# Cross attention: where the low part of the context rows is made, and when the sums of probabilities are taken

## The reference, cut to what matters

```
qx = _ln(qx, qxln_w, qxln_b)                      # 16 heads of 128, in 8 groups of 2
kvx = jnp.einsum('bsi,oi->bso', cond, w_kv_x)     # cond is the context
kx, vx = jnp.split(kvx, 2, axis=-1)
kx = _ln(kx.reshape(b, sc, g, d), kxln_w, kxln_b)
xout = _gqa(qx, kx, vx).reshape(b, s, nh * d)     # softmax(qx kx^T / sqrt(d)) vx
```

## Time and profile before

| | us |
|---|---|
| median of 3 runs | 2561.54 (2557.67 to 2563.57) |
| the profiled execution, its own time | 2560.54 |
| its span in the profile | 2558.5 |
| cross attention in it, first fold to last store, about | 1117 to 2315 |

### The profile page before, as it was taken

One profiled execution on the slowest core, in us unless ns is written; L12 is line 12 of the kernel. 1 busy time (PEld: TensorE's weight loads), 2 busy tenths in 40 slices (PEclk: granted clock), 3 DMA queues, 4 the chain that ended last, 5 costly groups with the idle time before them and its releaser, 6 DMA issues. The chain is left out here.

```text
span 2558.5 us, 38343 instructions
## 1 busy us (share of the span) xinstructions
PE 2341.7 (92%) x12603; PEld 2045.3 (80%) x12603; DVE 2019.6 (79%) x3952; ACT 1088.3 (43%) x1849; POOL 919.4 (36%) x640
## 2 busy tenths in 40 slices
PE   7999999999984788859999999999999999986797
PEld 6777777779983666658888888988888888976797
DVE  8999987877757887848888888888888888871487
ACT  1000001108855666614544554455545454554332
POOL 5455100200012344424545544555455444570000
PEclk9999999999996888879999999999999999997899
DMA  9667623517624010042222212222222112106211
GB/s 389 263 266 274 240 99 145 191 66 255 220 98 144 37 44 36 29 135 77 84 74 79 69 46 80 83 80 69 74 83 71 63 57 83 61 4 162 56 55 39
DMA packets 143384, 286.66 MB, mean 112 GB/s; under 512 B 26033, under 2 KB 114178, under 8 KB 139202
## 3 DMA queue, kind: packets, MB, share of 16 engines
q1 hardware_dynamic: 137266, 265.40, 30.0%
q0 software_dynamic: 6032, 20.20, 2.1%
HBM read 203.91 MB, written 81.66 MB: 112 GB/s over the span
## 5 line engine op out<-in xcount | busy, mean ns | idle before, releaser
L1697 POOL TENSOR_TENSOR s_acc<-s_acc,s_sx 125x896 f32<-125x896 f32 x128 | 275.8, 2154 | 261.3 <-DVE s_mxh L1941 114.6
L572 DVE BATCH_NORM_STATS2 s_st<-ps 125x6 f32<-125x128 f32 x1536 | 318.7, 280 | 55.6 <-PE ps L444 49.1
L1896 DVE TENSOR_TENSOR s_sx<-ps,keep_krs 125x896 f32<-125x896 f32 x192 | 208.9, 1088 | 167.3 <-PE ps L1807 164.1
L1761 ACT ACTIVATE s_sx<-s_sx 125x896 f32<-125x896 f32 x192 | 183.2, 954 | 352.8 <-DVE s_sx L1914 352.8
L1858 PE MATMUL ps<-s_p_hi,s_cn_hi 125*128 125x448 f32 x768 | 304.1, 396 | 6.6 <-DVE s_p_lo L1920 6.2
L1920 DVE TENSOR_TENSOR s_p_lo<-s_sx,s_p_hi 125x896 fp32r<-125x896 f32 x192 | 290.7, 1514 | 3.1 <-ACT s_p_hi L1766 3.1
L1807 PE MATMUL ps<-s_qc_hi,s_ct_hi 128*125 128x448 f32 x768 | 288.3, 375 | 1.3 <-DVE s_qc_lo L1879 1.3
L1858 PE MATMUL ps<-s_p_lo,s_cn_hi 125*128 125x448 f32 x768 | 285.1, 371 | 0.0
L1858 PE MATMUL ps<-s_p_hi,s_cn_lo 125*128 125x448 f32 x768 | 285.1, 371 | 0.0
L1807 PE MATMUL ps<-s_qc_lo,s_ct_hi 128*125 128x448 f32 x768 | 282.5, 368 | 0.0
L1807 PE MATMUL ps<-s_qc_hi,s_ct_lo 128*125 128x448 f32 x768 | 282.3, 368 | 0.0
(11 more groups left out here) (378 smaller groups left out, 5646.1 us busy)
## 6 DMA issues: line engine op xcount, KB each, us to landing
l_ahead<-in_ctxt SPq DMA_DIRECT2D x16, 1500.0 KB, 8.6
s_ct_hi<-ct_hi SPq DMA_DIRECT2D x48, 500.0 KB, 4.2
s_ct_lo<-ct_lo SPq DMA_DIRECT2D x48, 500.0 KB, 4.9
s_cn_raw<-in_ctx SPq DMA_DIRECT2D x48, 500.0 KB
l_raw<-in_ctxt SPq DMA_DIRECT2D x15, 1500.0 KB, 10.4
l_raw<-in_w SPq DMA_DIRECT2D x16, 1024.0 KB, 5.4
ct_hi<-l_hi SPq DMA_DIRECT2D x8, 1500.0 KB, 12.1
ct_lo<-l_lo SPq DMA_DIRECT2D x8, 1500.0 KB, 16.3
```

What stands on the lines that cost most here:

```text
L572: ins = dve.bn_stats(st[:, G * t + g, :], kx[0:TT, t % NB, g // 4, DH * (g % 4):DH * (g % 4) + DH])
L1697: pool.tensor_tensor(a, a, p[:, PR * w.pt:PR * w.pt + PR, :], ALU.add).then_inc(s["acc_ready"], 1)
L1761: act.activation(p, p, ACT.Exp).then_inc(s["exp_ready"], 1)
L1896: dve.tensor_tensor(by_group(sx[w.h][:, tiles, :]), by_group(sc[st % 2]), krs_b[:, tiles, HG * w.h:HG * w.h + HG].unsqueeze(3).to_broadcas ...
```

## The change

Four things are moved, all inside `cross_attention`; the computation is the same.

1. `cn_lo` is made by DVE at the end of steps 7, 9 and 11 instead of by POOL.
2. On PE the 12 value products of each step stand ahead of the sums, the broadcast and the product with the value weights of that step, not behind them.
3. On DVE the reciprocal of the sums stands at the very end of step `i` = 3 (behind `cn_lo`), and `ca` is made at `i` = 0 of the next unit instead of at `i` = 5.
4. On ACT `ut` stays at `i` = 3, `rdiag` moves to `i` = 4 and `rsc` to `i` = 5, each at the head of its step.

```
@@ steps_of @@
             body(B)
+            act(B + 1, 0)
             act(B + 1, 3)
@@ gpsimd @@
-                    c = cn_chunk(b, st)
-                    if c is not None:
-                        pool.wait_ge(s["cn_hi_ready"], NCH * b + c + 1)
-                        at = slice(CHT * c, CHT * c + CHT)
-                        pool.tensor_tensor(cn_lo[:, at, :], cn_raw[c][:, :, :], cn_hi[:, at, :].bitcast(F32), ALU.subtract).then_inc(s["cn_lo_ready"], 1)
@@ scalar @@
                     if w.i == 3 and w.two_back:
+                        act.wait_ge(s["pv_ready"], NPR * (w.u - 1))
...
+                        act.activation(ut[:, :, :, :].rearrange("p k g n -> p k (g n)"), pv, ACT.Copy).then_inc(s["ut_read"], 1)
+                    if w.i == 4 and w.two_back:
                         act.wait_ge(s["r4_ready"], w.u - 1)
...
                         ins.then_inc(s["rdiag_ready"], 1)
-                    if w.i == 3 and w.two_back:
-                        act.wait_ge(s["pv_ready"], NPR * (w.u - 1))
...
-                        act.activation(ut[:, :, :, :].rearrange("p k g n -> p k (g n)"), pv, ACT.Copy).then_inc(s["ut_read"], 1)
-                    if w.i == 4 and w.two_back:
+                    if w.i == 5 and w.two_back:
                         act.wait_ge(s["rb_ready"], w.u - 1)
@@ tensor: this block stands behind the mb product (i == 2) now, and not behind the value weights (i == 5) @@
+                    if w.has_v:
+                        pe.wait_ge(s["lo_ready"], w.v + 1)
...
+                        mm.then_inc(s["pv_ready"], 1)
                     if w.i == 3 and w.two_back:
                         pe.wait_ge(s["acc_ready"], NPR * (w.u - 1))
...
-                    if w.has_v:
-                        pe.wait_ge(s["lo_ready"], w.v + 1)
...
-                        mm.then_inc(s["pv_ready"], 1)
@@ vector @@
-                    if w.i == 3 and w.two_back:
-                        dve.wait_ge(s["sum_ready"], w.u - 1)
...
-                        dve.reciprocal(r4[:, :], sums).then_inc(s["r4_ready"], 1)
...
-                    if w.i == NPR - 1 and w.two_back:
-                        dve.wait_ge(s["rb_read"], w.u - 1)
-                        dve.wait_ge(s["v_ready"], w.u - 1)
+                    if w.i == 0 and w.three_back:
+                        dve.wait_ge(s["rb_read"], w.u - 2)
+                        dve.wait_ge(s["v_ready"], w.u - 2)
                         dve.tensor_tensor(ca[:, :], misc[:, 0:QH], rsc[:, :], ALU.mult).then_inc(s["v_read"], 1)
...
+                    c = cn_chunk(b, st)
+                    if c is not None:
+                        dve.wait_ge(s["cn_hi_ready"], NCH * b + c + 1)
+                        at = slice(CHT * c, CHT * c + CHT)
+                        dve.tensor_tensor(cn_lo[:, at, :], cn_raw[c][:, :, :], cn_hi[:, at, :].bitcast(F32), ALU.subtract).then_inc(s["cn_lo_ready"], 1)
+                    if w.i == 3 and w.two_back:
+                        dve.wait_ge(s["sum_ready"], w.u - 1)
...
+                        dve.reciprocal(r4[:, :], sums).then_inc(s["r4_ready"], 1)
```

More of the change, by code:

```diff
@@ L1738, in run @@
                     if w.i == 3 and w.two_back:
+                        act.wait_ge(s["pv_ready"], NPR * (w.u - 1))
+                        if not (static(b) and w.u < 3):
+                            act.wait_ge(s["v_ready"], w.u - 2)
+                        act.activation(ut[:, :, :, :].rearrange("p k g n -> p k (g n)"), pv, ACT.Copy).then_inc(s["ut_read"], 1)
+                    if w.i == 4 and w.two_back:
                         act.wait_ge(s["r4_ready"], w.u - 1)
@@ L1744, in run @@
                         ins.then_inc(s["rdiag_ready"], 1)
-                    if w.i == 3 and w.two_back:
-                        act.wait_ge(s["pv_ready"], NPR * (w.u - 1))
-                        if not (static(b) and w.u < 3):
-                            act.wait_ge(s["v_ready"], w.u - 2)
-                        act.activation(ut[:, :, :, :].rearrange("p k g n -> p k (g n)"), pv, ACT.Copy).then_inc(s["ut_read"], 1)
-                    if w.i == 4 and w.two_back:
+                    if w.i == 5 and w.two_back:
                         act.wait_ge(s["rb_ready"], w.u - 1)
@@ L1821, in run @@
                         pe.matmul(mb, ones_r[:, :], diag[:, :, :], start=True, stop=True).then_inc(s["mb_ready"], 1)
+                    if w.has_v:
+                        pe.wait_ge(s["lo_ready"], w.v + 1)
+                        if w.vt == 0 and not (static(w.vu) and w.vu < 1):
+                            pe.wait_ge(s["ut_read"], w.vu)
+                        if w.vh == 0 and PR * w.vt % CHT == 0:
+                            vb = b + (st - V_LAG) // STEPS
+                            pe.wait_ge(s["cn_lo_ready"], NCH * vb + PR * w.vt // CHT + 1)
+                        for j in range(PR):
+                            t = PR * w.vt + j
+                            for k in range(K2):
+                                c = 0
+                                for x, pp in ((cn_hi, (p_hi, p_lo)), (cn_lo, (p_hi,))):
+                                    for y in pp:
+                                        mm = pe.matmul(pv[:, k, :], x[:, t, k * P:k * P + P], y[w.vr][:, j, :],
+                                                       start=(t == 0 and c == 0), stop=(t == NT - 1 and c == 2))
+                                        c += 1
+                        mm.then_inc(s["pv_ready"], 1)
                     if w.i == 3 and w.two_back:
@@ L1904, in run @@
                         qc_split(w.u + 1, 1 - w.h, 0)
-                    if w.i == 3 and w.two_back:
-                        dve.wait_ge(s["sum_ready"], w.u - 1)
-                        if not (static(b) and w.u < 3):
-                            dve.wait_ge(s["rdiag_ready"], w.u - 2)
-                        dve.reciprocal(r4[:, :], sums).then_inc(s["r4_ready"], 1)
                     if w.has_p:
@@ L1946, in run @@
                             dve.tensor_tensor(mx[:, :], mxh[:, 0, :], mxh[:, 1, :], ALU.max).then_inc(s["mx_ready"], 1)
+                    c = cn_chunk(b, st)
[5 more added lines that the diff above has]
+                        dve.wait_ge(s["sum_ready"], w.u - 1)
+                        if not (static(b) and w.u < 3):
+                            dve.wait_ge(s["rdiag_ready"], w.u - 2)
+                        dve.reciprocal(r4[:, :], sums).then_inc(s["r4_ready"], 1)
                 steps_of(dve, None, run)
```

## The result

| | before | after |
|---|---|---|
| median, us | 2559.88 (2557.67 to 2563.57, 4 runs) | 2594.71 (2594.3 to 2602.53, 4 runs) |
| ratio to before | | 1.0142, 95% interval 1.0118 to 1.0165 |
| span of the profiled execution, us | 2558.5 | 2592.4 |

The changed kernel is slower by 1.4%. Forecast were 2597 us and a span of 2593.9.

What follows compares the result with a forecast made beforehand. PE's instruction list was taken to bound the kernel. Sums' waits -21, fold +15.0, broadcast +34.8, transposes +8.0, batch 0 +1.6, drain -7 and clock +4 gave +35, so 2597 us, range 2568 to 2620.

Steps and rivals of the forecast that it cites:

- The bound and the stop removed: PE's instruction list sets the time in cross attention; value products ahead of the sums remove their waits for `qc_lo`, -21 us.
- The rule of the ports: A DVE instruction with two SBUF inputs stands still until POOL's running instruction ends; moved `cn_lo` ends 1.10 us after the addition.
- The three stops: New PE losses per batch behind held `cn_lo`: fold of step 8 1.07 us, broadcast 2.32, transposes 0.53; 15.0, 34.8, 8.0 in all.
- Batch 0: Step 9's `cn_lo` holds back `p_lo` of step 10; value products wait some 2.4 us, a 0.8 wait goes: +1.6.
- The clock: PE's lower clock follows 8 of 15 broadcast stops and no longer follows the four old stalls: +4 us, bounds -8 and +27.
- The drain: After the last unit, 12 value products move into PE's 3.36 us wait for POOL: -7 us, bounds 3 and 9 off.
- What would show it: Signs: no sums' wait, fold waits 1 us, broadcast 2.3, DVE's `cn_lo` over 2 us long, POOL busy 130 us less.
- The sum: All terms over the whole kernel together: +35 us, span 2593.9, median 2597; chance 0.55.
- A: Rival: `cn_lo` on DVE isn't held, so fold and transposes lose nothing, broadcast 0.85 a batch; -23, 2538 us; chance 0.11.
- B: Rival: PE's clock falls after every long stall, 12 to 23 us more, 2609 to 2620 us; chance 0.20.
- D: Rival: nothing lost at fold and transposes, 1.7 at the broadcast, clock as now; within 5 us of 2561; chance 0.03.
- C: Rival: `cn_lo` slips ahead of POOL at step 11 (-8) and the clock doesn't fall (-12); 2577 us; chance 0.11.

## Why the prediction was right, point by point

**The bound and the stop removed** held. The sums' wait is gone. The gain of the new order by itself, -21 for the stops, -7 for the drain and -8 for the low clock behind the old stops, is -36; with `cn_lo` left on POOL -35.7 was measured. The terms didn't come out as well as their sum: in that kernel's trace the drain is 5.5 us shorter and the part ahead of it 32, where 7 and 29 were put.

**The rule of the ports** held, which was the step that carried the forecast. All three `cn_lo` of a batch ended 1.07 to 1.08 us after a POOL addition (forecast 1.10). The section Who interferes with whom of the Trainium skill's page SBUF — State Buffer agrees with it in both directions: POOL's additions took 2.95 to 3.17 us where DVE issued first. So these two engines meet at more than semaphores: none stands between `cn_lo` and the addition in the changed kernel.

**The three stops.** Fold: forecast 1.07, measured 1.09. Transposes: 0.53 and 0.57. Broadcast: 2.32 and 2.06. This last one is the term that was mis-sized, by 0.26 x 15 = 4 us. Counted from DVE's multiplication of step 9 (1380.02), POOL's addition ended 7.21 later where 7.29 was forecast, the reciprocal and `rdiag` behind `cn_lo` took 0.1 less than that, and PE, which would have started at 1389.71 - 2.06, came 0.07 later. Batch 0: the value products of step 11 lose 2.3 (2.4 forecast).

**The clock.** Forecast 8 of 15 stops at the broadcast followed by the lower level; counted 8 of 15 (8 of the 14 of the steady part, and not that of batch 15), and one more behind the value products' wait in batch 0. Busy time by stretch in the changed kernel, behind one stop each, columns as in Rows 1:

```profile
1315.00:1317.00 2.00, 2.00 (x7) 1.69 (x6) 1.72 (x2) 1.97 (x5) 0.12 (x1) 0.50 0.30 68
...
1465.80:1467.80 2.00, 2.00 (x10) 1.55 (x9) 2.00 (x3) 1.66 (x2) 0.29 (x1) 1.00 0.18 57
```

This number was a choice between ten rows below and two above. That it came out exact was luck, and the other kernels show how far it could have gone: 12 of 14 at 2.47 us. The Trainium skill's page TensorE: Matmul & The Clock Gate, section HAM oscillation — how this bites in real kernels, blames waits for transfers; the low stretches stand behind stops for `s_rdiag` here, so its reading (12 us less) stays refused.

**The drain** was mis-sized: -7 forecast, -4.5 measured. The two waits for POOL fell to one of 0.53, but a new one stands ahead of them. Timeline of PE in the drain of the changed kernel, which answers to the earlier trace rows:

```profile
2302.66 1.05 PE L1811 MATMUL ps<-keep_ident,s_mx 125*112 125x125 f32 x4 [4.13 <-DVE s_ca L1915]
2303.37 0.72 PE L1831 MATMUL ps<-s_p_hi,s_cn_hi 125*128 125x448 f32 x1
2303.89 0.57 PE L1831 MATMUL ps<-s_p_lo,s_cn_hi 125*128 125x448 f32 x1
```

`ca` is made one step later since the change, and behind batch 15 there are no score products to cover it. That is nearly all of this wait: with `cn_lo` left on POOL it is 4.69 us, and 3.58 where only the low part of step 11 is freed, so that the last held `cn_lo` (3.04 us) is about 0.5 of it. The move of `ca` was costed in the steady part and not in the drain.

**What would show it:** the signs named came as named, but for two sizes: POOL is busy 115 us less and not 130 (its 48 low parts had taken 129, but its other rows grew by 14, of which 12 are the last additions of the units), and the broadcast loses 2.06. **The sum** came out within 2 us (+35 against +33.9), partly by luck: the broadcast's term was 4 us too dear, and the drain's gain was put 2.5 too high.

**Rivals.** A's condition was made true in the kernel whose POOL waits, and gave 2537 where A said 2538. B is refused by 8 of 15, and D by the losses at fold and transposes. C's slip at step 11 happened in three other kernels, without the edit being meant for it; in the changed one it missed by 0.13 us.

**Open.** What makes the clock fall behind one stop and not behind the next of the same length. The terms of a batch add up to 4.71 us in the changed kernel (1.09 + 2.06 + 0.57 + 0.99) and 2.13 before (1.18, 0.35 and 0.6 for four low stretches of 2.1 in 14 batches); of these 2.58, 2.42 were measured, and the rest was not traced.

## What to carry to other kernels

Before an operation with two SBUF inputs is moved between DVE and POOL, ask which of the two engines issues first at its new place and who waits for the loser: the same move cost 1 us in one order and 71 in another. With the inputs made early as well, the kernel came out 7 us under the one that leaves the operation on POOL, though no kernel here has early inputs and `cn_lo` on POOL. Put such an operation where its inputs are long ready and behind, not ahead of, the small result that another engine waits for. The 1.09 us won ahead of a longer stop were mostly paid again at it (0.41 in the stop, 0.45 in the clock), so free the longest stop of a chain first.

## What the runs showed of the hardware that was not expected

- The hold is symmetric and decided by tenths of a microsecond. DVE's 1024 columns take 1.22 when first, and 1.31 to 3.07 when an addition is under way, by how much of it is left; POOL's 896 columns take 2.12 when first and 2.95 to 3.17 when DVE is.
- PE's stops and the lower clock, counted in one trace of each kernel: of the stops at the broadcast, none of 14 that lost 0.88 us (in two kernels), 8 and 10 of 14 that lost 2.06, and 12 of 14 that lost 2.47 were followed by it; of those at the fold (1.09), none; of those at the sums in the kernel before (1.18), 4 of 14.
